# Statistics moved into the tail of the block before, a double-buffered squaring loop, and two small transfers in place of two transposes, in a fused two-layer network on eight cores

## The reference

```python
x = x + LN(L0_attn(LN(x)))   # latent attention: gelu'd q, k; 16 heads of 64; rope on 2 heads; causal softmax
x = x + LN(L0_ffn(LN(x)))    # h = gelu(x @ T(W_fc).T); h = layernorm(h, ln_w, ln_b); h @ T(W_proj).T, width 4096
x = x + LN(L1_attn(LN(x)))   # q, k filtered in the spectrum of each head; full softmax, 16 heads of 64
x = x + LN(L1_ffn(LN(x)))    # three routed 16-leaf MLPs give q, k, v; one-head softmax attention of width 1024
```

## Time and profile before

| what | us |
|---|---|
| median of 2 runs | 12305.1 (12277.76 to 12332.44) |
| the profiled execution, its own time | 12310.32 |
| span of its slowest core (core 5), to which all rows refer | 12308.6 |
| spans of the eight cores | 12253.0 to 12308.6 |

### The profile page before, as it was taken

The page is one execution under the profiler, slowest core; times in us unless marked ns, Lnnn a source line. Parts: engine busy times, 40 slices in busy tenths (PEclk is TensorE's granted clock), DMA queues, the critical chain, the costliest instruction groups (busy, mean ns, idle before and its releaser), DMA issues.

```text
span 12308.6 us, 100831 instructions; the slowest of 8 cores (12253.0 to 12308.6 us)
## 1 busy us (share of the span) xinstructions
PE 7747.9 (63%) x31360; PEld 2873.4 (23%) x31360; DVE 2182.8 (18%) x4319; ACT 3740.2 (30%) x5047; POOL 1050.5 (9%) x1587
## 2 busy tenths in 40 slices
PE   5677205666558886374646776466655888836565
PEld 2111002333211111242422111133222111123343
DVE  3011541111200002311122112211130000041121
ACT  2354200111225554121222454211112555521122
POOL 0100001111010000101001000111101000010100
PEclk7555656777655556686766556677776555558777
DMA  1000433333100000000020000233320000001000
GB/s 41 1 4 17 146 123 111 117 117 117 19 5 2 2 2 10 15 15 14 1 64 5 2 3 10 72 117 117 116 59 7 1 3 2 9 8 21 14 1 28
DMA packets 251524, 472.71 MB, mean 38 GB/s; under 512 B 23552, under 2 KB 167936, under 8 KB 247936
## 3 DMA queue, kind: packets, MB, share of 16 engines
q0 software_dynamic: 90576, 256.00, 7.6%
q1 hardware_dynamic: 160432, 210.26, 5.3%
HBM read 478.93 MB, written 33.55 MB: 42 GB/s over the span
## 4 chain that ended last, share of the span: by engine, by line
PE 51%; DMA 14%; DVE 12%; ACT 10%; issue 7%; POOL 5%; DVEq 1%; ACTq 0%; POOLq 0%; SPq 0%
PE pall L109 50%; DMA arena<-w2q_dram 8%; ACT pt L119 5%; POOL pt L130 4%; ACT arena L119 3%; DVE st L157 2%; DVE arena L130 2%; PE pall L115 2%; DVE arena L154 2%; DVE arena L139 1%; DMA arena<-l0f_w2T 1%; ACT pall L119 1%; DVE stream L130 1%; DVE pt L154 1%; DVEq L54 1%
## 5 line engine op out<-in xcount | busy, mean ns | idle before, releaser
L109 PE MATMUL pall<-arena 128*128 128x256 bf16 (+7 forms) x19488 | 4746.9, 392 | 1368.1 <-DMA arena<-w2q_dram 648.2
L109 PEld LDWEIGHTS pall<-arena 128*128 128x128 bf16 (+3 forms) x19488 | 1816.2, 108 | 4101.3 <-issue 3522.7
L119 ACT ACTIVATE pt<-pall,cbias 128x1024 bf16<-128x1024 f32 (+7 forms) x2048 | 1926.5, 941 | 1856.3 <-PE pall L109 1833.4
L109 PE MATMUL pall<-pt,arena 128*65 128x512 bf16 (+5 forms) x6016 | 2072.1, 460 | 441.9 <-DVE pt L130 184.8
L119 ACT ACTIVATE arena<-pall 128x256 bf16<-128x256 f32 (+3 forms) x1160 | 534.5, 461 | 2962.9 <-PE pall L109 2818.9
L109 PEld LDWEIGHTS pall<-pt,arena 128*65 128x65 bf16 (+2 forms) x6016 | 558.9, 123 | 1891.1 <-issue 1834.6
L130 POOL TENSOR_TENSOR pt<-arena 128x256 bf16<-128x256 bf16 (+2 forms) x656 | 677.2, 1032 | 3605.4 <-ACT arena L119 2775.9
L115 PE MATMUL pall<-ident,pt 128*128 128x128 bf16 x1284 | 157.4, 306 | 904.0 <-DVE pt L154 675.1
L109 PE MATMUL pall<-pt,ones 128*1 128x256 bf16 (+2 forms) x896 | 339.2, 433 | 437.3 <-ACT pt L119 262.4
L130 DVE TENSOR_TENSOR arena<-pall,pt 64x1024 bf16<-64x1024 f32 x128 | 155.8, 1217 | 2528.8 <-ACT pt L119 2521.8
L109 PE MATMUL pall<-arena,pt 128*128 128x512 bf16 (+2 forms) x2112 | 429.2, 343 | 136.7 <-ACT pt L119 114.8
(11 more groups left out here) (103 smaller groups left out, 3242.8 us busy)
## 6 DMA issues: line engine op xcount, KB each, us to landing
arena<-wfcq_dram SPq DMA_DIRECT2D x128, 1024.0 KB
arena<-w2q_dram POOLq DMA_DIRECT2D x128, 1024.0 KB, 7.7
arena<-l0f_wfcT SPq DMA_DIRECT2D x8, 2048.0 KB
arena<-l0f_wfcT POOLq DMA_DIRECT2D x8, 2048.0 KB, 8.9
arena<-l0f_w2T SPq DMA_DIRECT2D x32, 512.0 KB
arena<-l0f_w2T POOLq DMA_DIRECT2D x32, 512.0 KB, 4.1
arena<-w2q_dram POOLq DMA_DIRECT2D x64, 256.0 KB, 2.8
y_out<-stream SPq DMA_DIRECT2D x4, 4096.0 KB
```

The lines of the kernel that those rows point to most:

```text
L109: return t.matmul(out, lhsT, rhs, start=start, stop=stop)
L119: self.do("scalar", lambda s: s.activation(out, in_, func, bias=bias, scale=scale, accum_out=accum_out), wait=wait, inc=inc)
```

## The change

1. A new function `emit_prenorm_stats` returns a callback that does the statistics of one tile of the next block's prenorm, and after every fourth tile the seven small operations for these four tiles. For L0 ffn, L1 attention and L1 ffn it is called from the tail of the block before (`tail_cb`), right after the tile's residual addition, and `emit_prenorm_fm` leaves out its first loop (`prelude=True`). L0 attention still runs the 16 callbacks at its start.
2. `emit_attention` has two squaring buffers, and PE's four matmuls of chunk c-1 are written behind POOL's squaring of chunk c.
3. In `emit_l0_ffn` the two transposes of `rrow_` and the two copies are gone. Two DMAs on the SyncE queue write the row's halves straight into the columns `st[:, 140]` and `st[:, 141]`.
4. The matmuls of the routed MLPs wait for the routing of their own two tiles rather than of all 16; the recomputation on ACT drops its wait for the routing of q.
5. The constant row of ones in `emit_b1_quantize` lies in another buffer and is written twice.

```diff
+def emit_prenorm_stats(p, h, tag, junk_bf):
+    def cb(t):
+        wt = p.req(f"strm{t}")
+        p.red(sums[:, t:t + 1], h.stream[:, t, :], ALU.add, wait=wt, inc="dve")
+        p.act(junk_bf[:, :], h.stream[:, t, :], AF.Square,
+              accum_out=ssq[:, t:t + 1], wait=wt, inc="act")
+        if t % 4 != 3:
+            return
+        q4 = t // 4
+        cs = slice(4 * q4, 4 * q4 + 4)
+        p.mark(f"{tag}_red{q4}", "dve"); p.mark(f"{tag}_sq{q4}", "act")
+        wv = p.req(f"{tag}_red{q4}", f"{tag}_sq{q4}")
+        p.ts("vector", mu[:, cs], sums[:, cs], 1.0 / D, None, ALU.mult, wait=wv, inc="dve")
+        p.tt("vector", nmu2[:, cs], mu[:, cs], mu[:, cs], ALU.mult, inc="dve")
+        p.ts("vector", veps[:, cs], ssq[:, cs], 1.0 / D, LN_EPS, ALU.mult, ALU.add, inc="dve")
+        p.tt("vector", veps[:, cs], veps[:, cs], nmu2[:, cs], ALU.subtract, inc="dve")
+        p.mark(f"{tag}_v{q4}", "dve")
+        p.act(rstd[:, cs], veps[:, cs], AF.Ln, wait=p.req(f"{tag}_v{q4}"), inc="act")
+        p.act(rstd[:, cs], rstd[:, cs], AF.Exp, scale=-0.5, inc="act")
+        p.mark(f"{tag}_rstd{q4}", "act")
+        p.stt("vector", negmur[:, cs], mu[:, cs], -1.0, rstd[:, cs],
+              ALU.mult, ALU.mult, wait=p.req(f"{tag}_rstd{q4}"), inc="dve")
+        p.mark(f"{tag}_nm{q4}", "dve")
+    return cb
...
@@ emit_prenorm_fm, second loop
-              wait=p.need(tag + "_rstd", tag + "_nm", f"{tag}_cast{par}"), inc="act")
+              wait=p.need(f"{tag}_rstd{t // 4}", f"{tag}_nm{t // 4}",
+                          f"{tag}_cast{par}"), inc="act")
...
@@ emit_attention
+        for c in range(8):
+            par = c % 2
+            p.tt("gpsimd", sqs[par], X[:, c, :], X[:, c, :], ALU.mult,
+                 wait=list(qk_ready) + p.need(f"{tag}_nc{par}"), inc="gp")
+            p.mark(f"{tag}_sqc{par}", "gp")
+            if c > 0:
+                nc_mms(c - 1)
+        nc_mms(7)
...
@@ emit_outproj_postnorm and emit_postnorm_tile
         p.mark(f"strm{t}", "dve")
+        if tail_cb is not None:
+            tail_cb(t)
...
@@ emit_b3_fff
-    selw = p.req(f"b3sel{seq}{f}")
...
+        tg = (sel_off + g * 256) // 128
+        selw = p.req(f"b3sel{seq}{f}_T{tg}", f"b3sel{seq}{f}_T{tg + 1}")
...
@@ emit_l1_ffn
-                  wait=stream_ready(p) + p.need("b3rg_hi") +
-                  p.req(f"b3sel{seq}q"), inc="act")
+                  wait=stream_ready(p) + p.need("b3rg_hi"), inc="act")
...
@@ emit_b1_quantize
-    onesrow32 = h.f32a[0:1, 0:128]
-    p.memset("vector", onesrow32, 1.0, wait=p.need("blkend"), inc="dve")
-    p.mark("q_ones", "dve")
+    onesrow32 = bbuf.bitcast(F32)[0:1, 0:128]
...
@@ emit_l0_ffn, end of a group
         for t2 in range(2):
-            p.transp(pbank(h, 6 + t2, 1)[:, 0:1],
-                     rrow_[0:1, t2 * 128:(t2 + 1) * 128], h.idf32[:, :],
-                     wait=p.req("b1r", "consts_gp") + p.bkw(6 + t2, 1),
-                     inc="pe")
-        p.mark("b1rT", "pe")
-        for t2 in range(2):
-            p.copy("vector", st[:, 140 + t2:141 + t2],
-                   pbank(h, 6 + t2, 1)[:, 0:1],
-                   wait=p.req("b1rT") if t2 == 0 else (), inc="dve")
-            p.bkr(6 + t2, 1, "dve")
-        p.mark("b1rcols", "dve")
+            p.dma("sync", st[:, 140 + t2:141 + t2],
+                  rrow_[0:1, t2 * 128:(t2 + 1) * 128],
+                  wait=p.req("b1r") + p.need("b1rcols_used"))
+        p.mark("b1rcols", "dsp")
```

More of the change, by code:

```diff
@@ L474, in emit_prenorm_fm @@
     negmur = st[:, 96:112]
-    jnk = h.junk if junk_ap is None else junk_ap
-    for t in range(NT):
+    def cb(t):
         wt = p.req(f"strm{t}")
-        p.red(sums[:, t:t + 1], h.stream[:, t, :], ALU.add, wait=wt, inc="dve")
-        p.act(jnk[:, :], h.stream[:, t, :], AF.Square,
+        p.red(sums[:, t:t + 1], h.stream[:, t, :], ALU.add, wait=wt,
+              inc="dve")
+        p.act(junk_bf[:, :], h.stream[:, t, :], AF.Square,
               accum_out=ssq[:, t:t + 1], wait=wt, inc="act")
-    p.mark(tag + "_red", "dve"); p.mark(tag + "_sq", "act")
@@ L482, in emit_prenorm_fm @@
[L482 to L492, removed]
@@ L493, in emit_prenorm_fm @@
-    p.mark(tag + "_nm", "dve")
+        if t % 4 != 3:
[4 more added lines that the diff above has]
+        wv = p.req(f"{tag}_red{q4}", f"{tag}_sq{q4}")
+        p.ts("vector", mu[:, cs], sums[:, cs], 1.0 / D, None, ALU.mult,
+             wait=wv, inc="dve")
+        p.tt("vector", nmu2[:, cs], mu[:, cs], mu[:, cs], ALU.mult, inc="dve")
+        p.ts("vector", veps[:, cs], ssq[:, cs], 1.0 / D, LN_EPS,
+             ALU.mult, ALU.add, inc="dve")
@@ new lines, in cb @@
+        p.tt("vector", veps[:, cs], veps[:, cs], nmu2[:, cs], ALU.subtract,
+             inc="dve")
+        p.mark(f"{tag}_v{q4}", "dve")
+        p.act(rstd[:, cs], veps[:, cs], AF.Ln, wait=p.req(f"{tag}_v{q4}"),
+              inc="act")
+        p.act(rstd[:, cs], rstd[:, cs], AF.Exp, scale=-0.5, inc="act")
+        p.mark(f"{tag}_rstd{q4}", "act")
+        p.stt("vector", negmur[:, cs], mu[:, cs], -1.0, rstd[:, cs],
+              ALU.mult, ALU.mult, wait=p.req(f"{tag}_rstd{q4}"), inc="dve")
@@ new lines, in cb, with emit_prenorm_fm @@
+        p.mark(f"{tag}_nm{q4}", "dve")
+    return cb
+def emit_prenorm_fm(p, h, xnfm, tag, lo_cb=None, junk_ap=None,
+                    prelude=False):
+    st = h.st32
+    sums = st[:, 0:16]; ssq = st[:, 16:32]; mu = st[:, 32:48]
+    nmu2 = st[:, 48:64]; veps = st[:, 64:80]; rstd = st[:, 80:96]
+    negmur = st[:, 96:112]
+    if not prelude:
+        jnk = h.junk if junk_ap is None else junk_ap
+        cb = emit_prenorm_stats(p, h, tag, jnk)
+        for t in range(NT):
+            cb(t)
@@ L744, in emit_attention, with nc_mms @@
         ps = pbank(h, 0, 4)[0:16, 0:2048]
[L745 to L748, removed]
+        def nc_mms(c):
+            par = c % 2
             for nq in range(4):
@@ L1250, in emit_b3_sel @@
         p.mark(f"{tag}_tp{par}", "dve")
+        p.mark(f"{tag}_T{t}", "dve")
     p.mark(tag, "dve")
@@ L1511, in emit_postnorm_tile, with emit_l1_ffn @@
     p.mark(f"strm{t}", "dve")
-def emit_l1_ffn(p, h, seq):
+    if tail_cb is not None:
+        tail_cb(t)
+def emit_l1_ffn(p, h, seq, prelude=False):
     arn = h.arn
@@ L1696, in emit_b1_quantize @@
         acc = st[:, 366:367]
+        p.memset("vector", onesrow32, 1.0, wait=p.need("blkend"), inc="dve")
+        p.mark("q_ones", "dve")
         for c in range(nch):
```

60 lines of the change are left out of this document (37 added, 23 removed).

## The result

| kernel | us, median (lowest to highest) | to before, with 95% interval |
|---|---|---|
| before | 12294.6 (12268.6 to 12350.4) | 1 |
| after | 12230.6 (12199.9 to 12317.2) | 0.9945 [0.9923, 0.9967] |
| forecast | 12280 (12220 to 12400) | 0.998 |

What follows compares the result with a forecast made beforehand. No engine was taken to bound the whole kernel: each stage's last-ending chain counts. From 12310.3 us, -128 + 23 + 46 - 7 + 33 + 5 = -28 and half the 5 us to the median gave 12280, range 12220 to 12400.

Steps and rivals of the forecast that it cites:

- Squarings: Score bound: with two buffers POOL squares without a stop beside PE's matmuls, 60 gaps shortened, -128 us.
- Attention tails and their starts: Statistics moved into four attention tails cost 122 us, against 99 saved at the next blocks' starts: +23 us.
- The rival that the statistics hide: Idle time of DVE and ACT in tails and boundaries covers the added statistics: 12067 us (-1.9%), chance 0.05.
- L0 ffn: Group boundaries: callbacks less the saved L1 attention start +46, POOL's squaring -7, small DMAs +33 us.
- Small DMAs: L0 ffn group ends: two serial DMAs of 2.2 us start the scaling 4.6 us after Exp, 16 x 2.1 = +33 us.
- Callbacks: L0 ffn boundary: added statistics delay the next Gelu by 3.9 us, or 5.6 on every second group.
- the rival of slow DMAs: L0 ffn group ends: small DMAs take 6.6 us each, giving 12423 us (+0.9%), chance 0.15.
- POOL's relief: L0 ffn: POOL's first squaring of a group no longer runs beside DVE's residual addition, 14 x 0.5 = -7 us.
- I cost the delay at nothing: L0 ffn: the next group's first weight load, queued behind the small DMAs, stays covered; 112 us without the cover.
- L0 attention start: Prenorm at its start now has four small chains; the third costs 2.3 us on both sequences, +5 us.
- Routing waits, ones row: Loosened routing waits gain nothing; the ones row costs one 128-wide memset of 0.2 us more.
- The clock: Rival: a denser score bound raises the clock in L1's attention core; a quarter of the most gives 12019 us, chance 0.03.

Runs made afterwards that it cites:

- a_norm: The kernel before with only the double-buffered squaring of the score bound added; 12187.6 us, 0.9891 of before.
- h_place: The changed kernel with the same statistics placed where DVE and ACT wait, in attention tails and L0 ffn groups; 12033.3 us, 0.9748 of before.
- b_dma: The kernel before with only the two small DMAs in place of the two transposes; 12346.8 us, 1.0001 of before.
- c_spwait: The kernel before with each later group's first load of the first weight waiting for the previous group's Exp; 12305.2 us, 0.9958 of before.
- d_order: The changed kernel with the next group's first weight load written ahead of the two small DMAs on SyncE; 12322.4 us, 1.0006 of before.
- g_tr: The changed kernel with the two transposes and copies back in place of the small DMAs; 12292.0 us, 0.9961 of before.
- i_exact: h_place with transposes back, second-weight loads issued two chunks earlier and matmuls waiting for their own load alone; 11464.8 us, 0.9312 of before.

## Why the prediction was right, and where it was not

*Squarings.* -128 forecast, -125 in the stages, -134 in a_norm. Period forecast 3.70, measured 3.74.

*Attention tails and their starts.* +23 forecast; measured +106 - 85 = +21 (the sixteenth tile's part is in the starts). The period of 8.69 was forecast as 8.7. The rival that the statistics hide falls for the place that the change gives them, and its reason stands: h_place shows that DVE and ACT had the idle time. What lies between the two is the place of the new sum and the new square, not the work.

*L0 ffn.* With the callbacks and the saved start the forecast was +46 - 7 + 33 = +72, measured is +73 - 39 = +34. Term by term:
- Small DMAs: scaling 4.4 us after Exp, forecast 4.6; +1.8 us each, forecast +2.1. They go out 2.0 us apart, near the 2.2 that I took, and not at the 6.6 of the row beside a 4 MB load: the rival of slow DMAs (0.15) falls. The Trainium skill ("DMA: Bandwidth & Descriptors", Anatomy of one DMA) has a fixed cost of about 2.0 us for each DMA, fitted on GpSimd's path. The trace agrees on SyncE's queue: 2.06 and 2.01 from issue to next issue.
- Callbacks: Gelu 28.4 and 30.3 after Exp, forecast 28.8 and 30.5. Some 4 us less in all, small DMAs included.
- POOL's relief, -7: the first two steps of a group are 1.1 us shorter, 14 x 1.1 = -15. POOL's first squaring did become 0.60 us in place of 1.14, as forecast; but b_dma has the shorter steps without it. The term was too small, and its cause isn't supported; the steps go with the granted clock.
- **The failed step is "I cost the delay at nothing".** I had asked what the late weight load does to its own matmuls, and there the answer holds: PE waits for it, 7.9 us on the mean and 10.1 at most, under ACT's 28 to 30. I hadn't asked what it does to the load that it used to fly beside. Over the 14 ends with a next group that load lands in 5.9 us instead of 7.6, PE waits for it 3.4 us instead of 5.1, and the step is 2.3 us shorter, a missing term of 14 x 2.3 = -32. c_spwait shows it alone, d_order and g_tr take it away, b_dma has it, and before has the short step where no group follows. By the landings of all the loads (last section) 1 us between the two issues would do as well as 20; no run tried that. The prediction did name the companion, under the small DMAs, and drew only that they would be quicker.

With it, the sum is -28 - 32 - 8 (short first steps) - 4 = -72, against -65 in the stages and -67 measured; the five steps between the first two and the last are 0.4 us longer in sum, 6 us over the 16 groups.

The time fell into the range because the range is 180 us wide and the two large terms, the squarings and the tails, were right. The forecast gain of 28 us was less than half of the measured one, and the missing term alone is larger than the whole forecast. The small difference that was forecast came from terms that nearly cancel, so its sign was not safe.

*L0 attention start:* +5 forecast, +4.6. *Routing waits, ones row:* the stage from the last residual to the end of the apply loop in L1 ffn goes by the saved loop alone (-22 of 25 less the 3.6 moved there). They weren't tried by themselves.

*The clock.* In the L1 core 0.50 before and after, the lower of the two levels (1.2 and 2.4 GHz), with PE busy 87% of 1198 us, and 1199 us in a_norm: the denser score bound ahead of it does nothing. By the Trainium skill ("TensorE: Matmul & The Clock Gate", Part 1) recent activity releases the higher level. In this stage the measurement differs: the level stays the lower one nearly to its end.

## What to carry to other kernels

When an edit delays a transfer, ask two things: who waits for it, and what was on the way at the same time; the second can be worth more. Work that is added to a chain costs by its place: put it where its engine waits for another one, since the same sum costs 1.3 us in front of the chain's next link and next to nothing behind it. And where PE waits for loads over and over at 34% use of the DMA engines, look at which load the wait counts before blaming the bandwidth.

## What the runs showed of the hardware

- A 1 MB load of the second weight lands in 5.9 us alone, and in 7.8 on the mean when the other queue's 1 MB load is issued 0.3 to 0.5 us behind it (5349 loads in nine kernels). At 0.7 to 0.9 us behind it is 6.3, and from 1 to 2.4 us 6.0 (some 800 loads), though the two must still overlap; in i_exact, at some 4 us, 6.1 to 6.2. In these loads the time goes with how close together the two are issued. No run moved a load by 1 us alone, so that the spacing is the cause is not shown.
- Two DMAs of 128 pieces of 4 bytes, SBUF to SBUF, the second waiting for the first, go out 2.06 us apart, and the next load on the queue 2.01 us behind the second (after).
- The clock records of the profiles have a third value beside 0.5 and 1.0 of the full clock, 0.81, in some cores and executions of before and of changed kernels alike. L1 ffn's last part takes 567 to 573 us without it and up to 624 with it, 0.13 us more for each us at 0.81. What sets it was not tried.
